# Fewer filler matmuls per attention step (rate 3 to rate 2) in an eight-core attention and FFN layer

## The reference, cut to what matters

```python
Q, K, V = proj(Wq), proj(Wk), proj(Wv)          # x @ W.T, split into 16 heads of 64
O = causal_softmax(Q @ K.T / 8) @ V             # online softmax over blocks of 128
x = layernorm(x + O @ Wo.T)
h = silu(x @ (w_gate/127).T) * (x @ (w_up/127).T)   # hidden 3072
x = layernorm(x + h @ (w_down/127).T)
```

## Time and profile before

| | |
|---|---|
| time, median of 2 runs | 2058.33 us (2056.78 to 2059.88) |
| the profiled execution: its own time | 2056.15 us |
| span of its slowest core (core 7), first to last instruction | 2055.1 us |
| spans of the eight cores | 2031.6 to 2055.1 us |
| TensorE matmul busy | 1619.7 us, 79% |
| ScalarE busy | 828.0 us, 40% |
| VectorE busy | 611.8 us, 30% |
| mean granted TensorE clock, as a share of full speed | 0.862 (core 7) |

### The profile page before, as it was taken

The page is one execution under the profiler, slowest core; times in us unless marked ns, Lnnn a source line. Parts: engine busy times, 40 slices in busy tenths (PEclk is TensorE's granted clock), DMA queues, the critical chain, the costliest instruction groups (busy, mean ns, idle before and its releaser), DMA issues. The chain is left out here.

```text
span 2055.1 us, 22780 instructions; the slowest of 8 cores (2031.6 to 2055.1 us)
## 1 busy us (share of the span) xinstructions
PE 1619.7 (79%) x7240; PEld 616.6 (30%) x7240; DVE 611.8 (30%) x1436; ACT 828.0 (40%) x999; POOL 183.8 (9%) x221
## 2 busy tenths in 40 slices
PE   3857988779888699887677665768998879998862
PEld 1512333223332133331111112323443334443320
DVE  1334233342332623324412112463111121112124
ACT  0025766657664577663377760341111011112022
POOL 1010000100001000001000001001221112220000
PEclk9968999879998699995588876968999999999985
DMA  7791233452242522340000004324776648776622
GB/s 98 118 134 21 42 48 56 58 77 42 42 62 42 73 42 45 51 71 3 2 1 1 1 1 89 92 47 42 77 76 66 64 48 76 72 73 66 87 56 82
DMA packets 224112, 115.31 MB, mean 56 GB/s; under 512 B 152030, under 2 KB 215520, under 8 KB 224000
## 3 DMA queue, kind: packets, MB, share of 16 engines
q0 software_dynamic: 215104, 96.94, 38.7%
q1 hardware_dynamic: 8896, 16.91, 2.5%
HBM read 201.66 MB, written 8.65 MB: 102 GB/s over the span
## 5 line engine op out<-in xcount | busy, mean ns | idle before, releaser
L415 ACT ACTIVATE pt<-sp,cbias 128x1024 bf16<-128x1024 f32 (+3 forms) x640 | 623.3, 986 | 360.7 <-PE sp L403 348.6
L443 PE MATMUL op<-pt,vbuf 128*65 128x512 bf16 (+3 forms) x1280 | 377.0, 379 | 125.6 <-DVE pt L424 55.7
L398 PE MATMUL sp<-qbuf,kbuf 64*128 64x512 bf16 (+3 forms) x640 | 238.1, 381 | 2.1 <-DVE cbias L324 2.1
L403 PE MATMUL sp<-qbuf,kbuf 64*128 64x512 bf16 (+3 forms) x640 | 238.3, 381 | 0.0
L841 PE MATMUL gps<-x1b,wgb 128*128 128x512 bf16 x768 | 187.9, 389 | 26.2 <-DVE x1b L809 13.0
L899 PE MATMUL dps<-hbuf,wdd 128*128 128x512 bf16 x768 | 179.2, 392 | 35.4 <-DVE y L910 34.1
L443 PEld LDWEIGHTS op<-pt,vbuf 128*65 128x65 bf16 x1280 | 121.4, 117 | 267.2 <-issue 223.8
L850 PE MATMUL ups<-x1b,wub 128*128 128x512 bf16 x768 | 184.7, 384 | 6.8 <-DVE hbuf L862 6.8
L858 ACT ACTIVATE sgb<-gps 128x512 bf16<-128x512 f32 x96 | 57.3, 597 | 308.4 <-PE gps L841 298.9
L226 PE MATMUL pp<-xstg,wkb 128*128 128x512 bf16 x512 | 149.5, 410 | 40.0 <-DMA xstg<-xfm 40.0
L240 PE MATMUL pp<-wvb,xstg 128*128 128x256 bf16 x1024 | 163.4, 280 | 0.6
(11 more groups left out here) (83 smaller groups left out, 1215.2 us busy)
## 6 DMA issues: line engine op xcount, KB each, us to landing
xstg<-xfm POOLq DMA_DIRECT2D x32, 1024.0 KB, 9.2
xstg<-xq POOLq DMA_DIRECT2D x16, 1024.0 KB, 8.4
wgb<-wgT POOLq DMA_DIRECT2D x48, 256.0 KB, 4.7
wub<-wuT POOLq DMA_DIRECT2D x48, 256.0 KB, 5.6
wdd<-wdT POOLq DMA_DIRECT2D x16, 768.0 KB, 8.6
xres<-xq SPq DMA_DIRECT2D x32, 256.0 KB, 3.3
yout<-y SPq DMA_DIRECT2D x4, 2048.0 KB, 6.9
wqb<-wqT POOLq DMA_DIRECT2D x4, 512.0 KB, 7.9
```

What stands on the lines that cost most here:

```text
L398: nc.tensor.matmul(sp[buf][:, js * 128: 512], kbuf[pb][0:64, hp * T + kb * 128: hp * T + kb * 128 + 128], qbuf[pb][0:64, hp * TOWN + qbase ...
L403: s_s.inc(nc.tensor.matmul(sp[buf][:, 512 + js * 128: 1024], kbuf[pb][64:128, hp * T + kb * 128: hp * T + kb * 128 + 128], qbuf[pb][64:128 ...
L415: s_exp.inc(nc.scalar.activation(pview, sview, AF.Exp, bias=cbias[pb][:, 0:1]))
L443: lastpv = nc.tensor.matmul(ops[hl][:, js * 128: 512], vbuf[pb][:, kb * VGW + (2 * hp + hl) * 65: kb * VGW + (2 * hp + hl) * 65 + 65], pt[ ...
```

## The change

One argument changes: in each step of `attention_pass`, `fill` pulls 2 yields of the filler and not 3.

```diff
@@ -499,7 +499,7 @@
             if p >= 1:
                 parts.append(norm_gen(p - 1))
             filler = chaing(*parts) if parts else None
-            filler = attention_pass(p, filler, rate=3)
+            filler = attention_pass(p, filler, rate=2)
             if filler is not None:
                 for _ in filler:
                     pass
```

## The result

The changed kernel takes 2138.49 us (median of 11 runs), the kernel before 2061.32 us in the runs beside it (10 runs); the ratio is 1.037, 95% interval 1.034 to 1.039. It is slower, by some 77 us. The profiled execution took 2131.44 us, with core 7 again the slowest at 2130.4 us; the forecast for an execution like that of before was 2132.8, rounded to 2133.

A forecast was written before the change was run, and what follows sets the result against it. TensorE bounds K-filler steps; V steps lie just over the 1.17 us ring of matmuls and exponential. Passes 0 to 2 with tails, normalisation and gaps add 27.6, 27.0 and 23.0 us, pass 3 -1: 2056.15 + 76.6 = 2132.8, say 2133 us (2094 to 2160).

The forecast's parts named there:

- (a): 96 full-width steps of a pass: from 127.5 to 115.2 us, 12.3 us less.
- (b): Eight groups of eight masked steps in a pass: about 4 us less.
- (c): Waits at bank starts and masks hide two fillers instead of three, clock may drop: 3.3 us lost per pass.
- The lower bound of 6 us saved: Passes 0 to 2: a third of the filler may be worth only 6 us, judged from pass 3 without filler.
- (d): Leftover projections behind passes 0 to 2, waiting on two-slot x loads: 41 us, between 37.8 and 44.
- the unaccompanied stretch: Start of the kernel, where `proj_gen(0)` runs alone; the same work there gave 44 us for the tail.
- (e): Normalisation moves behind the projections in passes 1 and 2, at about its own price: 20.3 us.
- (f): Gap behind the tail: 27.4 us, as after the start's projections, against 28.75 us before.
- The sum: Stage totals 287.7, 308.0 and 308.0 us for passes 0 to 2, pass 3 1 us less: +76.6 us.
- The tail of 29 us: Rival behind the passes: tail's loads are hidden; from 29 us down within 2%, 2098 us; chance 0.07.
- All matmul time comes back: Rival in the passes: 23 us saved per pass, 2103 us, or 2088 with a 36 us tail; chance 0.14.
- the first rival: The pass hardly shortens: 6 us saved instead of 13, 2154 us, or 2163 with a 44 us tail; chance 0.16.

The follow-up runs named there:

- the second kernel: Burst in each bank's first step plus four x buffers, with reciprocals moved to after 240 yields and normalisation matmuls 48 yields later; ratio 0.986 to the kernel before.

## Why the prediction was right, point by point

The time, the sign and the mechanism came out: 2133 forecast, 2131.4 in the like execution, 2138.5 as the median. That the slowest core came within 2 us is in part luck, but the size is not: the span grew by 76.4 us as a mean over the eight cores, and 76.6 was forecast.

- **(a) Full-width steps.** Two K at 1.29 us and two V at 1.17 were forecast; 1.29 and 1.16 were measured. On core 7 the full-width parts of pass 0 sum to 128.7 us against 143.3 (they hold the banks' starts too): 14.6 less, 12.3 forecast; as means over the cores 11.3 less.
- **(b) Masked steps.** 85.4 us against 88.0 in pass 0: 2.7 less instead of 4, and 2.7 less as a mean over the cores too. The group that I put at 11.5 us took 13.4, 12.2 and 11.4 us in passes 0, 1 and 2.
- **(c) The allowance of 3.3 us** for hidden filler and a lower clock was too much: the clock stayed at 0.92 to 0.94 in the passes. They took 214.0 to 217.0 us on core 7 where I had 218.3, and 216.7, 215.8 and 214.4 as means over the cores. The lower bound of 6 us saved, taken from pass 3, was far off; that pass 3 itself ran at a clock of 0.78 may be why, but no run shows it.
- **(d) The tail** was the term sized too small: 41 us forecast, 42.8 to 45.8 measured on core 7, 43.3 as a mean over passes and cores. I had left out the 1.78 us for which TensorE waits at the beginning, since VectorE empties the accumulators before it empties `pp`; the rest is near the 44 us of the unaccompanied stretch, which was the better guide than the estimate below it. The rule on bursts and DMA waits of the Trainium skill, "TensorE: Matmul & The Clock Gate", section "HAM oscillation - how this bites in real kernels", named the mechanism: the two bursts behind waits of 7.75 and 8.45 us, longer than a burst of 3.61, did start slow. But I had stretched it to all four bursts, and misread when I said that one of four stays fast. Two did, there as here: the first, at 3.61 us, and the third, which follows the second without a wait, so that the pair takes 9.76 us at the start and 8.97 us in the tail.
- **(e) Normalisation** 21.3 and 22.6 us against 20.3, its wait 8.66 us in pass 1 and not 6.57. **(f) The gap** 27.1 to 28.0 us against 27.4.
- **The sum.** The errors of (c) and (d) go in opposite directions, 1 to 4 us each per pass, and cancel in part. Each of the three stage totals is within 3 us of its forecast (286.9 for 287.7, 310.4 for 308.0, 308.9 for 308.0). Together they came out 2.5 us too dear on core 7 (+80.1 for +77.6), and what follows pass 2 took 5.5 us less where 1 was forecast: that these cancel too, and leave 1.4 us, is chance.
- **The rivals.** The tail of 29 us, from which the change would have stayed within 2%, was reached only by adding buffers, and the kernel then took 2061 us. (By its own sum that rival gives 2097 us and not 2098; nothing hangs on it.) *All matmul time comes back* asked for passes under 210 us; one of the 24, 209.2 us, was that short. No pass took over 225, as the first rival asked.

The term on which the sign hung was the tail, and it could be read off a stretch of the same code in the trace of before.

## What to carry to other kernels

Before thinning out filler, ask where the remainder goes and what covers its loads there: a two-deep buffer that is ample at 20 us per slice starves at 3.6 us per slice. Filler is worth most in the waits that exist anyway: here the same 128 matmuls cost 23 us as lumps in busy steps and 1 to 4 us in the first steps of the banks, seven of which hold a wait of about 2.2 us. The Pool queue issued its transfers in program order here, so that one that waited 42.48 us for a computation held back the loads behind it.

## What the runs showed of the hardware that was not expected

- The gain from covering the banks' waits, 22 us a pass, was larger than the waits, 15.9 us: behind a wait of some 2 us TensorE often ran at 1.2 GHz (behind five of seven in pass 0 of the kernel before, six of seven with the lump in key block 3, on core 7), though it had hardly waited before it (0.32 us before the wait of 2.12 us in the kernel before, 0.59 us before that of 2.22 us), and over a pass the granted clock was 0.93. With the lump in the wait, the idle time left in it was 1.32 us and the clock over the pass was 1.00.
- The start profits from four x buffers by 20 to 22 us, as means over the cores, with no fewer bytes: the DMA share rose from 0.78 to 1.06.
- The f32 normalisation matmuls, whose weights have two rows, took about 1.7 us each (two records) behind the pass, at the lower clock, and 0.85 us at the full clock within it. The granted clock fell while they ran, at 557.06 us on core 5 of the second kernel, although TensorE had not been idle since 552.93.
